# A second norm's end shared among three engines, a later last maximum, and a re-ordered first stage in an attention and mixture-of-experts kernel

## The chip, the cores and the metric

One core of a Trainium2 chip. The metric is device time in microseconds (us) of one execution. The kernel before took 849.73 us, the median of 3 runs (847.44 to 850.27).

## The reference, cut to what matters

x is [32, 256, 128] in fp32: 32 batches of 256 rows. The kernel holds it as 64 tiles of 128 rows.

```python
xn = layernorm(x)                                     # the first norm
q, k, v = split(xn @ w_qkv)                           # 16 heads of 8
attn = softmax(causal(q k^T / sqrt(8)))
y = (attn v) @ w_proj + b_proj + xn
a = (y - mean(y)) * rsqrt(var(y) + 1e-5) * gamma + beta   # the second norm
probs = softmax(xn @ Wr)                              # 8 experts, the best 2
f = sum over the best 2 of prob * (gelu(xn @ W1 + b1) @ W2 + b2)
out = x + a + f
```

## The kernel before

There are three stages. **The first** normalises x. VectorE takes moments of each tile (`tiles_moments`, `moments`), GpSimd raises the variance to -1/2 (L555) in the five column ranges of `MOMENTS`, and VectorE makes offsets. ScalarE normalises groups 0 to 11 (four tiles each, L729), VectorE groups 12 to 15 (L755). TensorE transposes each group; ScalarE takes the fp16 high part (L640), VectorE the low part (`low_group`, L760); TensorE multiplies by the router's weights (L1089). `step(0, 0)`, the q and k of batch 0, lies between. GpSimd then adds beta into x_all in eight pieces of eight tiles (L567), each as soon as its groups are normalised. `picks` finds the best two experts of each row and `places` gives each row a slot; both are chains of small VectorE operations, `places` after step 1. SyncE, in program order: the rows of q and k of batch 0 to DRAM (L462) and back re-laid (`load_half`: q_diag L437, k_cat L438), then in step 1 `fill_slots` (16 transfers of 598.5 KB that clear the slots in DRAM), two biases and two pieces of the experts' weights, and only then the q and k rows of step 1 (L462) and their return.

**The second** is software-pipelined attention: steps 1 to 35, of which a step s projects batch s (PROJECT), takes row maxima of batch s-1 (MAXIMA), exponentials of batch s-2 (SOFT), sums and the second norm's measures of batch s-3 (FINISH), and the norm's end of batch s-4 (LAST). Steps 4 to 23 are a hardware loop of two; from 24 (`TAIL`) they are written out, since they also load and split pieces of the experts' weights. In a step every engine follows the order of `USES`. Its end, before:

```python
("head", "onT", FINISH), ("wide1", "s3", SOFT), ("maxA", "m10", MAXIMA),
("wide0", "s4", SOFT), ("maxB", "m11", MAXIMA), ("head", "o0", SOFT),
("misc", "shift", MAXIMA), ("wide1", "s5", SOFT), ("head", "proj", FINISH),
```

The first word is the PSUM buffer: a use must wait until the one before it in that buffer has been read out. m0 to m11 are scores for maxima (TensorE L1127, L1131; VectorE reduces them, L911), s0 to s5 scores for exponentials (TensorE L1113, L1117; ScalarE L653; GpSimd masks them, L581), o0 and o1 the value products (TensorE L1148; ScalarE reads them out, L671), shift the transposed maxima (ScalarE L649, then four SyncE transfers, L478), oT0, oT1 and onT transposes, proj the output product (L1196). o0 needs masks s0 to s2, o1 (in the next step) s3 to s5. After proj VectorE runs `add_and_measure` (L936 to L945), GpSimd the -1/2 power (L608). VectorE's `last`, placed after shift, ends the norm of the batch before: two L951, y2 = (x2 - mean) * gamma, and two L957, x_all += y2 * rstd. GpSimd also sends rows to their slots (`send_tile`, two L572 a tile): from step 2 on one tile at "m0" and one at "s2"; in the tail every even step three, at "m0", "s1", "s3". At the end of step 3 VectorE runs `pack_experts` (L884 to L898). In the tail ScalarE takes the high part of a piece (L681) at the end of a step and VectorE the low part (L982) before `add_and_measure`.

**The third** runs 72 tiles of 256 slots through the experts and adds the parts to x_all, which goes out.

## Time and profile before

| | |
|---|---|
| median of 3 runs | 849.73 us |
| the profiled execution | 851.77 us |
| its span | 850.0 us |
| busy: PE / VectorE / ScalarE / GpSimd | 699.9 / 692.9 / 525.4 / 536.0 us |
| first stage to the last router product | 0 to 63.9 us |
| attention steps | about 64 to 558 us |
| experts' tiles, then the last sum | to 811 us, to 850 us |

Durations are of the one profiled execution; 1.77 us of its time lie outside its span. A row gives the start, the duration of the whole group (with xN for N instructions), the engine, the line, and in brackets the idle time before it and what ended that. A row's duration is longer than the spacing of neighbours where operations overlap at their ends. PE is TensorE, PEld its weight load, DVE VectorE, ACT ScalarE, POOL GpSimd, SPq the SyncE queue.

### The profile page before, as it was taken

How to read it: one execution, taken by the hardware profiler on the slowest of the kernel's cores; microseconds unless marked ns; L12 is line 12 of the kernel's file. 1: busy time of each engine (PE TensorE's matmuls, PEld its weight loads, DVE VectorE, ACT ScalarE, POOL GpSimd, SP SyncE). 2: the span in 40 equal slices, each digit the busy share in tenths (PEclk: the TensorE clock that was granted, in tenths of full speed). 3: DMA queues.
4: the chain of work that ended last, by engine and by line, in shares of the span. 5: the costliest groups of instructions: out<-in, count | busy, mean ns of one | idle time of the engine just before them, and what ended most of it. 6: DMA issues, size and time to landing. Idle time of an engine off the chain costs nothing.

```text
span 850.0 us, 24989 instructions
## 1 busy us (share of the span) xinstructions
PE 699.9 (82%) x7877; PEld 518.1 (61%) x7878; DVE 692.9 (82%) x1617; ACT 525.4 (62%) x1039; POOL 536.0 (63%) x575
## 2 busy tenths in 40 slices
PE   1366579999999999999888888868999999999800
PEld 1243346666666666666655555537888889888800
DVE  5778878898999998989889999557788888888744
ACT  4541346565656565656556565537989999999800
POOL 8750456767676776767777777334767676667710
PEclk9999899999999999999999999978999999999955
DMA  8294122232323232232233432202222222222189
GB/s 220 80 400 122 64 84 94 81 111 79 114 77 111 80 111 94 94 98 90 84 127 107 139 125 78 64 7 62 84 85 80 85 88 84 82 82 82 56 266 335
DMA packets 113313, 93.66 MB, mean 110 GB/s; under 512 B 16618, under 2 KB 97650, under 8 KB 113268
## 3 DMA queue, kind: packets, MB, share of 16 engines
q1 hardware_dynamic: 95508, 70.26, 27.0%
q0 software_dynamic: 8704, 18.17, 5.9%
q10 hardware_dynamic: 9056, 4.66, 1.9%
q8 instruction: 25, 0.41, 0.2%
q14 instruction: 20, 0.16, 0.1%
HBM read 43.85 MB, written 48.93 MB: 109 GB/s over the span
## 4 chain that ended last, share of the span: by engine, by line
PE 56%; DVE 13%; issue 7%; POOL 7%; DMA 6%; ACT 5%; SPq 5%; DVEq 0%; ACTq 0%; POOLq 0%
PE wide L1259 10%; PE bank_head L1148 7%; PE wide L1113 5%; PE bank_head L1250 5%; PE bank_maxB L1250 5%; PE bank_maxA L1127 4%; PE bank_maxB L1127 3%; DMA xn_rows<-parts_dram 3%; DMA k_cat<-qk_rows 3%; DVE shift L911 3%; POOL probs L581 3%; PE bank_misc L1173 3%; SPq L478 2%; PE bank_maxB L1131 2%; PE bank_maxA L1131 2%
## 5 line engine op out<-in xcount | busy, mean ns | idle before, releaser
L581 POOL TENSOR_SCALAR_AFFINE_SELECT probs<-probs 128x512 f32<-128x512 f32 (+1 forms) x192 | 158.3, 833 | 103.6 <-ACT probs L653 102.8
L653 ACT ACTIVATE probs<-wide 128x1024 f32<-128x1024 f32 x192 | 188.8, 1018 | 47.3 <-PE wide L1117 24.5
L619 POOL DMA_INDIRECT parts_dram<-o_T,dest x144 | 161.0, 1118 | 74.7 <-issue 48.6
L572 POOL DMA_INDIRECT x_slots<-xn_rows,slot_i x128 | 127.3, 995 | 62.8 <-DVE slot_i L868 31.4
L911 DVE TENSOR_REDUCE shift<-bank_maxA 128x2 f32<-128x512 f32 (+1 forms) x192 | 132.1, 688 | 20.1 <-PE bank_maxA L1131 12.9
L911 DVE TENSOR_REDUCE shift<-bank_maxB 128x2 f32<-128x512 f32 (+1 forms) x192 | 131.5, 685 | 4.9 <-PE bank_maxB L1131 0.8
L687 ACT ACTIVATE probs<-wide,b_all 128x256 f32<-128x256 f32 x288 | 121.4, 478 | 16.8 <-PE wide L1259 10.0
L1148 PE MATMUL bank_head<-probs,v_aug 128*32 128x256 f32 (+1 forms) x2048 | 98.9, 334 | 19.1 <-POOL probs L581 18.9
L1259 PE MATMUL wide<-xgT_raw,xnT 128*128 128x256 f16 x864 | 109.2, 277 | 3.7 <-DVE xgT_raw L1020 3.6
L1003 DVE TENSOR_TENSOR probs<-probs 128x512 f16<-128x512 f32 x144 | 99.7, 692 | 5.5 <-ACT probs L693 1.1
L1127 PE MATMUL bank_maxA<-k_cat,q_diag 128*128 128x128 f16 (+1 forms) x512 | 76.2, 252 | 28.5 <-DVE shift L911 19.5
L1148 PEld LDWEIGHTS bank_head<-probs,v_aug 128*32 128x32 f32 x2048 | 60.5, 111 | 56.2 <-issue 21.4
L1259 PEld LDWEIGHTS wide<-xgT_raw,xnT 128*128 x864 | 78.8, 99 | 16.4 <-issue 4.9
L671 ACT ACTIVATE o_T<-bank_head 128x512 f32<-128x512 f32 x64 | 38.2, 597 | 73.8 <-PE bank_head L1148 73.8
L1113 PE MATMUL wide<-q_diag,k_cat 128*128 128x512 f16 x256 | 76.9, 384 | 0.0
L1127 PE MATMUL bank_maxB<-k_cat,q_diag 128*128 128x256 f16 (+1 forms) x512 | 75.5, 250 | 0.3
L1127 PEld LDWEIGHTS bank_maxA<-k_cat,q_diag 128*128 128x128 f16 x512 | 36.7, 98 | 56.2 <-DVE shift L911 34.4
L1127 PEld LDWEIGHTS bank_maxB<-k_cat,q_diag 128*128 128x128 f16 x512 | 42.2, 99 | 30.3 <-DVE shift L911 8.0
L1131 PE MATMUL bank_maxB<-mask,ident 128*128 128x256 f16 (+1 forms) x192 | 60.5, 315 | 0.0
L1131 PE MATMUL bank_maxA<-mask,ident 128*128 128x256 f16 (+1 forms) x192 | 60.4, 314 | 0.0
L1250 PE MATMUL bank_head<-xnT,probs 128*128 x864 | 55.3, 220 | 0.0
L1250 PE MATMUL bank_maxB<-xnT,probs 128*128 x864 | 55.0, 219 | 0.2 <-DVE probs L1003 0.2
(174 smaller groups left out, 1252.4 us busy)
## 6 DMA issues: line engine op xcount, KB each, us to landing
qk_rows<-split SPq DMA_DIRECT2D x32, 512.0 KB, 3.2
x_slots<-fill SPq DMA_DIRECT2D x16, 598.5 KB, 7.6
fill<-x_slots SPq DMA_DIRECT2D x72, 133.0 KB
q_diag<-qk_rows SPq DMA_DIRECT2D x256, 32.0 KB
k_cat<-qk_rows SPq DMA_DIRECT2D x64, 128.0 KB
xn_rows<-parts_dram SPq DMA_DIRECT2D x8, 1024.0 KB, 11.8
x_all<-in_x SPq DMA_DIRECT2D x8, 512.0 KB, 7.6
pieces_f<-in_w SPq DMA_DIRECT2D x8, 512.0 KB, 4.8
```

The source lines that it names most:

```text
L572: pool.indirect_dma_start(out=x_slots, out_offset=bass.IndirectOffsetOnAxis(ap=slot_i[:, t, c:c + 1], axis=0), in_=xn_rows[:, t, :], in_of ...
L581: pool.affine_select(out=part, in_=part, compare_op=ALU.is_ge, fill=0.0, base=0, pattern=[[0, n], [1, P]], channel_multiplier=-1).then_inc ...
L619: pool.indirect_dma_start(out=parts_dram, out_offset=bass.IndirectOffsetOnAxis(ap=dest[:, of, t:t + 1].bitcast(U32), axis=0), in_=y[:, of ...
L653: act.activation(probs[:, u, :], ps[:, :], ACT.Exp, scale=SCALE).then_inc(empty, 1)
L687: act.activation(hT[:, par, c, :], wide[par][:, S * c:S * (c + 1)], ACT.Gelu, bias=b1_all[:, bass.ds(e, 1), c:c + 1].rearrange("p a b -> p ...
L911: V.tensor_reduce(dst, ps[:, :].rearrange("p (j k) -> p j k", j=nh), axis=AX.X, op=ALU.max, negate=True).then_inc(empty, 1)
L1113: last = M(ps[:, 512 * h2:512 * (h2 + 1)], keys[:, gs[0], :], q_diag[:, par, gs[0], 2 * h2:2 * h2 + 2, :], start=True, stop=True)
L1127: M(ps[:, keys * n_:keys * (n_ + 1)], q_diag[:, 1 - par, g, j, P * qt:P * (qt + 1)], k_cat[:, 1 - par, g, 0:keys], start=(n_ == 0), stop=F ...
L1131: M(dst, ident16[:, :], mask16[:, :].rearrange("p (o k) -> p o k", o=1).to_broadcast([P, nh, P]), start=False, stop=True, skip_group_check ...
L1148: last = M(dst, v_aug[:, of, kt, J * g + j, :], p_, start=(kt == 0), stop=(kt == 1), skip_group_check=True)
L1250: last = M(results[:, D * t:D * (t + 1)], hT_parts[:, par, hp, c, P * t:P * (t + 1)], w2_parts[:, wp_, bass.ds(e_2, 1), c, :].rearrange("p ...
L1259: last = M(wide[par][:, S * c:S * (c + 1)], w1_parts[:, wp_, bass.ds(e_1, 1), P * c:P * (c + 1)].rearrange("p a d -> p (a d)"), xgT[:, par ...
```

## The change

GpSimd's first memset of q_diag is split in two, the ranges of the moments become six (the third is eight tiles), ScalarE normalises 13 groups, VectorE three. `low_router` and `step(0, 0)` come later on VectorE. The router's and wqkv's weights have semaphores of their own, the router's are loaded first. The beta adds move: four pieces after `picks`, two at the end of step 2, two at the end of step 3. In `places` eight scans over 64 elements become one over 512, and four operations go into `weights`, at the end of step 2. Sends begin in step 3 and go on to step 32; an even tail step has two tiles at "m0", one at "s2". s5 comes before o0. At the end of a step ScalarE multiplies y2 by rstd (two operations) and GpSimd adds y2 into x_all (one of 128x256), in place of the two L957. High parts of pieces are taken right after v.

```diff
+        goes_on = probs[:, 5, 512:1024].rearrange("p (e t) -> p e t", e=E)
         is_top16, key16 = (probs[:, 4, NT * E // 2 * u:NT * E // 2 * (u + 1)].bitcast(BF16).rearrange("p (t e) -> p t e", e=E) for u in range(2))
         pick16 = probs[:, 5, 0:NT * E].bitcast(BF16).rearrange("p (c t e) -> p c t e", c=2, e=E)
         top = sb("top", [P, 2, NT])
@@ -169,6 +172,8 @@
...
@@ -240,7 +246,7 @@
 
...
-            ("wide0", "s4", SOFT), ("maxB", "m11", MAXIMA), ("head", "o0", SOFT),
-            ("misc", "shift", MAXIMA), ("wide1", "s5", SOFT), ("head", "proj", FINISH),
+            ("wide0", "s4", SOFT), ("maxB", "m11", MAXIMA), ("wide1", "s5", SOFT),
+            ("head", "o0", SOFT), ("misc", "shift", MAXIMA), ("head", "proj", FINISH),
...
-                places = ("m0", "s1", "s3") if (s - TAIL) % 2 == 0 else SEND_AFTER
+                places = ("m0", "m0", "s2") if (s - TAIL) % 2 == 0 else SEND_AFTER
...
-        ACT_GROUPS = 12
+        ACT_GROUPS = 13
...
-        MOMENTS = [(0, 8), (8, 16), (16, 32), (32, 48), (48, 64)]
-        assert NT == 64 and 4 * ACT_GROUPS == MOMENTS[-1][0]
...
+        MOMENTS = [(0, 8), (8, 16), (16, 24), (24, 40), (40, 56), (56, 64)]
...
-            pool.memset(q_diag[:, 0, :, :, :], 0.0).then_inc(consts, 1)
             for c, (begin, end) in enumerate(MOMENTS):
+                if c < 2:
+                    pool.memset(q_diag[:, 0, 2 * c:2 * c + 2, :, :], 0.0).then_inc(consts, 1)
...
+                elif c == 2:
                     pool.memset(q_diag[:, 1, :, :, :], 0.0).then_inc(consts, 1)
-                elif c == 2:
+                elif c == 3:
...
-            for c in range(BETA_PARTS):
+            pool.memset(goes_on[:, :, :], 1.0).then_inc(consts, 1)
...
+            pool.memset(goes_on[:, :, 0], 0.0).then_inc(consts, 1)
+
+            def add_beta(c):
                 tiles_ = slice(NT // BETA_PARTS * c, NT // BETA_PARTS * (c + 1))
-                wait_normed(pool, 2 * c + 1)
                 pool.tensor_tensor(x_all[:, tiles_, :], x_all[:, tiles_, :],
-                                   beta_bc[:, :].rearrange("p (o d) -> p o d", o=1).to_broadcast([P, NT // BETA_PARTS, D]), ALU.add).then_inc(offset_ready, 1)
+                                   beta_bc[:, :].rearrange("p (o d) -> p o d", o=1).to_broadcast([P, NT // BETA_PARTS, D]),
+                                   ALU.add).then_inc(offset_ready if c < BETA_PARTS - 1 else res_ready, 1)
+
+            wait_normed(pool, ACT_GROUPS - 1)
+            wait_normed(pool, GROUPS - 1)
+            pool.wait_ge(weights_loaded, 64)
+            pool.wait_ge(route, ROUTE_PICKED + 1)
+            for c in range(BETA_PARTS // 2):
+                add_beta(c)
...
-                    pool.wait_ge(route, ROUTE_DONE)
+                    pool.wait_ge(route, ROUTE_WEIGHTS)
...
+                if s in (2, 3):
+                    for c in range(2 * s, 2 * s + 2):
+                        add_beta(c)
+                if has(s, LAST):
+
+                    b = s - LAST
+                    pool.wait_ge(y2_scaled, b * QT + QT)
+                    mine = x_all[:, b * QT:(b + 1) * QT, :]
+                    pool.tensor_tensor(mine, mine, y2[:, :, :], ALU.add).then_inc(res_ready, 1)
...
-            act.dma_start(wqkv[:, :], w_qkv).then_inc(weights_loaded, 16)
+            act.dma_start(wr[:, :], w_router).then_inc(router_loaded, 16)
+            act.dma_start(wqkv[:, :], w_qkv).then_inc(qkv_loaded, 16)
             act.dma_start(wp[:, :], w_proj).then_inc(weights_loaded, 16)
-            act.dma_start(wr[:, :], w_router).then_inc(weights_loaded, 16)
...
-            act.wait_ge(weights_loaded, 96)
+            act.wait_ge(qkv_loaded, 16)
...
                         act.activation(v_aug[:, 1 - par, :, :, 0:HD],
                                        ps[:, 0:QT * D].rearrange("p (t h d) -> p t h d", t=QT, h=H), ACT.Copy).then_inc(empty, 1)
+                        for i in pieces(s):
+                            high_piece(i)
...
                         exp(s, int(what[1:]))
-                for i in pieces(s):
-                    act.wait_ge(piece_loaded[i % 2], 16 * (i // 2 + 1))
-                    act.activation(part_of(i, 0), piece[i % 2], ACT.Copy).then_inc(piece_high, 1)
+                if has(s, LAST):
+
+                    b = s - LAST
+                    act.wait_ge(rstd2_ready, b * 1 + 1)
+                    act.wait_ge(y2_ready, b * QT + QT)
+                    for t in range(QT):
+                        act.activation(y2[:, t, :], y2[:, t, :], ACT.Copy, scale=rstd2[:, t:t + 1]).then_inc(y2_scaled, 1)
...
-                then(V.tensor_scalar(xn_rows[:, :, D + 4], best[:, 0, :], -1.0, float(E), ALU.mult, ALU.add))
...
-                for e in range(E):
-                    V.tensor_tensor_scan(place[:, :, e], ones[:, :], total.rearrange("p (t e) -> p t e", e=E)[:, :, e],
-                                         padded[:, e:e + 1], ALU.mult, ALU.add).then_inc(route, 1)
-                    route_count += 1
-                dve.wait_ge(exp_router, 2)
-                then(V.tensor_reduce(red[:, :], prob[:, :, :], axis=AX.X, op=ALU.add))
...
+                then(V.tensor_tensor(first_tile_total, first_tile_total, padded[:, :], ALU.add))
+                dve.wait_ge(consts, 31)
+                then(V.tensor_tensor_scan(place_by_expert[:, :, :].rearrange("p e t -> p (e t)"), goes_on[:, :, :].rearrange("p e t -> p (e t)"), total, 0.0,
+                                          ALU.mult, ALU.add))
...
-                then(V.reciprocal(xn_rows[:, :, D], red[:, :]))
-                then(V.tensor_tensor(red[:, :], top[:, 1, :], xn_rows[:, :, D], ALU.mult))
-                then(V.tensor_tensor(xn_rows[:, :, D + 2], red[:, :], xn_rows[:, :, D], ALU.subtract))
...
+            def weights():
+
+                nonlocal route_count
+                dve.wait_ge(exp_router, 2)
+                then(V.tensor_reduce(red[:, :], prob[:, :, :], axis=AX.X, op=ALU.add))
+                V.tensor_scalar(xn_rows[:, :, D + 4], best[:, 0, :], -1.0, float(E), ALU.mult, ALU.add).then_inc(route, 1)
+                route_count += 1
+                then(V.reciprocal(xn_rows[:, :, D], red[:, :]))
+                then(V.scalar_tensor_tensor(out=xn_rows[:, :, D + 2], in0=top[:, 1, :], scalar=-1.0, in1=xn_rows[:, :, D],
+                                            op0=ALU.add, op1=ALU.mult))
...
+                if has(s, LAST):
+                    dve.wait_ge(y2_ready, (s - LAST) * QT + QT)
                 V.tensor_tensor(x2[:, :, :], ps[:, 0:QT * D].rearrange("p (t d) -> p t d", t=QT), xpb[:, :, :], ALU.add).then_inc(empty, 1)
...
+                dve.wait_ge(res_ready, b * 1 + 1)
                 for t in range(QT):
                     V.scalar_tensor_tensor(out=y2[:, t, :], in0=x2[:, t, :], scalar=mv2[:, t, 0:1], in1=gamma_bc[:, :],
                                            op0=ALU.subtract, op1=ALU.mult).then_inc(y2_ready, 1)
-                dve.wait_ge(rstd2_ready, b * 1 + 1)
-                for t in range(QT):
-                    dve.wait_ge(y2_ready, b * 2 + (t + 1))
-                    mine = x_all[:, bass.ds(b * QT + t, 1), :].rearrange("p a d -> p (a d)")
-                    V.scalar_tensor_tensor(out=mine, in0=y2[:, t, :], scalar=rstd2[:, t:t + 1], in1=mine,
-                                           op0=ALU.mult, op1=ALU.add).then_inc(res_ready, 1)
...
+                if isinstance(s, int) and s == SOFT:
+                    weights()
...
-            step(0, 0)
-            tiles_moments(56, 64)
...
-            dve.wait_ge(rstd_ready, 5)
...
+            low_group(5)
+            tiles_moments(56, 64)
+            offsets(4)
+            moments(5)
+            low_group(6)
+            step(0, 0)
+            low_group(7)
+            dve.wait_ge(rstd_ready, 6)
+            half_of_mean(ACT_GROUPS)
...
-            dve.wait_ge(offset_ready, BETA_PARTS)
...
+                for n_, (counting, order_) in enumerate(((after16, "p t e -> p (t e)"), (ones16, "p t e -> p e t"))):
...
+                        last = M(wide[1][:, 512 * n_:512 * (n_ + 1)], counting[:, :], pick16[:, c, :, :].rearrange(order_),
...
+            pe.wait_ge(weights_loaded, 64)
...
```

## Rows read from the trace of the kernel before

**Rows 1.** Windows, loop: PE, PEld, DVE, ACT, POOL busy us, clock, DMA share, GB/s.
```profile
190.00:414.00 224.00, 218.72 (x2372) 144.50 (x2370) 204.13 (x449) 138.31 (x193) 162.03 (x193) 1.00 0.30 96
```

**Rows 2.** Timeline, first stage, where the beta adds run.
```profile
36.30 9.24 POOL L567 TENSOR_TENSOR x_all<-x_all,beta_bc 128x1024 f32<-128x1024 f32 x4
38.71 7.16 DVE L755 TENSOR_SCALAR xn_rows<-x_all,mean,rstd 128x128 f32<-128x128 f32 x4
46.40 1.10 DVE L755 TENSOR_SCALAR xn_rows<-x_all,mean,rstd 128x128 f32<-128x128 f32 x4
```

**Rows 3.** Timeline, VectorE from picks to the first maxima of steps 1 and 2.
```profile
63.98 0.69 DVE L825 TENSOR_REDUCE top<-wide 128x64 f32<-128x512 f32 x1 [0.58 <-PE wide L1089]
71.41 0.69 DVE L911 TENSOR_REDUCE shift<-bank_maxA 128x4 f32<-128x512 f32 x1
84.27 2.02 DVE L850 TENSOR_TENSOR_SCAN probs<-ones,padded,wide 128x64 f32<-128x64 f32 x8
91.67 0.69 DVE L911 TENSOR_REDUCE shift<-bank_maxA 128x4 f32<-128x512 f32 x1
```

**Rows 4.** Timeline, SyncE's queue over the same time.
```profile
39.89 18.64 SPq L423 DMA_DIRECT2D x_slots<-fill  x16
...
66.79 2.01 SPq L416 DMA_DIRECT2D pieces_f<-in_w  x2
73.57 0.37 SPq L462 DMA_DIRECT2D qk_rows<-split  x1
76.36 1.75 SPq L437 DMA_DIRECT2D q_diag<-qk_rows  x4
```

**Rows 5.** Timeline, step 4: TensorE's wait while VectorE runs `pack_experts`.
```profile
125.09 0.39 PE L1127 MATMUL bank_maxA<-k_cat,q_diag 128*128 128x256 f16 x2 [3.89 <-DVE shift L911]
```

**Rows 6.** The chain that ended last, one step of the loop: start, us, what.
```profile
316.43 1.44 PE bank_head L1148 x32
317.86 0.32 PE bank_misc L1181 x2
318.18 0.43 PE wide L1117 x2
318.61 0.69 PE bank_head L1196 x4
...
324.03 0.39 PE bank_maxA L1127 x2
```

**Rows 7.** Timeline, ScalarE, GpSimd and VectorE in the same step.
```profile
315.38 1.94 ACT L653 ACTIVATE probs<-wide 128x1024 f32<-128x1024 f32 x2
317.93 0.60 ACT L671 ACTIVATE o_T<-bank_head 128x512 f32<-128x512 f32 x1 [0.61 <-PE bank_head L1148]
319.42 0.42 DVE L936 TENSOR_TENSOR x<-bank_head,xpb 128x256 f32<-128x256 f32 x1 [0.46 <-PE bank_head L1196]
319.81 1.09 POOL L581 TENSOR_SCALAR_AFFINE_SELECT probs<-probs 128x1024 f32<-128x1024 f32 x1 [0.37 <-ACT probs L653]
```

**Rows 8.** Waits from 95 to 420 us: total us, times, longest.
```profile
PEld bank_head L1196 <- ACT o_T L671: 10.3, 22, 0.5
PE bank_head L1148 <- POOL probs L581: 6.8, 21, 1.2
```

**Rows 9.** Groups: the first two from 190 to 414 us, the third over the span.
```profile
L957 DVE SCALAR_TENSOR_TENSOR x_all<-y,rstd,x_all 128x128 f32 x32 | 21.5, 710 | 0.0
L590 POOL TENSOR_TENSOR xpb<-xn_rows,bproj_bc 128x256 f32<-128x256 f32 x16 | 10.8, 678 | 0.0
L729 ACT ACTIVATE xn_rows<-x_all,offset,rstd 128x128 f32<-128x128 f32 x48 | 19.6, 483 | 2.5 <-DVE offset L800 2.5
```

**Rows 10.** Tail steps: the chain, then TensorE's timeline.
```profile
454.88 3.99 DMA k_cat<-qk_rows
...
479.28 1.51 PE L1148 MATMUL bank_head<-probs,v_aug 128*32 128x256 f32 x32 [1.07 <-POOL probs L581]
485.01 1.29 PE L1148 MATMUL bank_head<-probs,v_aug 128*32 128x256 f32 x24 [1.32 <-POOL probs L581]
```

More of the change, by code:

```diff
@@ L109, in attention_and_moe @@
         piece = (pieces_f32[:, 0, :], pieces_f32[:, 1, :])
-        others, place, rank, prob = (probs[:, u, 0:NT * E].rearrange("p (t e) -> p t e", e=E) for u in range(4))
+        others, place, rank = (probs[:, u, 0:NT * E].rearrange("p (t e) -> p t e", e=E) for u in range(3))
+        place_by_expert = probs[:, 3, 0:NT * E].rearrange("p (e t) -> p e t", e=E)
+        prob = sb("prob", [P, NT, E])
+        goes_on = probs[:, 5, 512:1024].rearrange("p (e t) -> p e t", e=E)
         is_top16, key16 = (probs[:, 4, NT * E // 2 * u:NT * E // 2 * (u + 1)].bitcast(BF16).rearrange("p (t e) -> p t e", e=E) for u in range(2))
@@ L171, in attention_and_moe @@
         x_loaded = [sem(f"x_loaded{c}") for c in range(2 * CHUNKS)]
+        router_loaded = sem("router_loaded")
+        qkv_loaded = sem("qkv_loaded")
         weights_loaded = sem("weights_loaded")
@@ L382, in attention_and_moe @@
         EXPERTS_PACKED = 16
[L383 to L385 removed]
+        ROUTE_DONE = 27
+        ROUTE_WEIGHTS = 31
+        MOMENTS = [(0, 8), (8, 16), (16, 24), (24, 40), (40, 56), (56, 64)]
+        assert NT == 64
         EARLY_AFTER = 4
@@ L653, in exp, with high_piece @@
                 act.activation(probs[:, u, :], ps[:, :], ACT.Exp, scale=SCALE).then_inc(empty, 1)
+            def high_piece(i):
+                act.wait_ge(piece_loaded[i % 2], 16 * (i // 2 + 1))
+                act.activation(part_of(i, 0), piece[i % 2], ACT.Copy).then_inc(piece_high, 1)
             def step(s, par):
@@ L839, in places @@
                 V.tensor_tensor(top[:, 1, :], top[:, 1, :], top[:, 0, :], ALU.subtract).then_inc(less_top, 1)
-                then(V.tensor_scalar(xn_rows[:, :, D + 4], best[:, 0, :], -1.0, float(E), ALU.mult, ALU.add))
                 dve.wait_ge(route_counts, 1)
                 total = wide[1][:, 512:1024]
-                then(V.tensor_reduce(padded[:, :], total.rearrange("p (t e) -> p e t", e=E), axis=AX.X, op=ALU.add))
+                then(V.tensor_reduce(padded[:, :], total.rearrange("p (e t) -> p e t", e=E), axis=AX.X, op=ALU.add))
                 then(V.tensor_scalar(padded_i[:, :], padded[:, :], float(S - 1), None, ALU.add))
@@ L1026, in tile, with half_of_mean @@
                     low_hidden(s - 1, 1 - par, 1)
+            def half_of_mean(c):
+                nonlocal prep_count
+                V.tensor_scalar(mean[:, 4 * c:], mean[:, 4 * c:], 0.5, None, ALU.mult).then_inc(prep, 1)
+                prep_count += 1
+                dve.wait_ge(prep, prep_count)
             tiles_moments(0, 8)
@@ L1034, in _ @@
             moments(1)
-            tiles_moments(16, 24)
+            tiles_moments(16, 20)
             offsets(1)
-            tiles_moments(24, 32)
+            low_router()
+            tiles_moments(20, 24)
             moments(2)
+            tiles_moments(24, 28)
             low_group(0)
+            offsets(2)
+            tiles_moments(28, 32)
+            low_group(1)
             tiles_moments(32, 40)
-            offsets(2)
-            low_group(1)
-            tiles_moments(40, 48)
             moments(3)
             low_group(2)
-            tiles_moments(48, 56)
+            tiles_moments(40, 48)
             offsets(3)
             low_group(3)
-            step(0, 0)
-            tiles_moments(56, 64)
+            tiles_moments(48, 56)
             moments(4)
             low_group(4)
-            dve.wait_ge(rstd_ready, 5)
-            cols = slice(*MOMENTS[4])
-            V.tensor_scalar(mean[:, cols], mean[:, cols], 0.5, None, ALU.mult).then_inc(prep, 1)
-            prep_count += 1
-            dve.wait_ge(prep, prep_count)
+            low_group(5)
[7 more added lines that the diff above has]
+            half_of_mean(ACT_GROUPS)
             for g in range(ACT_GROUPS, GROUPS):
                 normalise_group(g)
-                low_group(g - ACT_GROUPS + 5)
-            for g in range(GROUPS - ACT_GROUPS + 5, GROUPS):
+                low_group(g - ACT_GROUPS + 8)
+            for g in range(GROUPS - ACT_GROUPS + 8, GROUPS):
                 low_group(g)
             picks()
-            dve.wait_ge(offset_ready, BETA_PARTS)
             steps(dve, step, after=((), (places,)), first_tile=lambda: tile(0, 0, None))
             tiles(dve, tile, load=False, begun=1)
+            dve.wait_ge(res_ready, B + 1)
             for c in range(LAST_CHUNKS):
@@ L1096, in count_picks @@
                 pe.wait_ge(route, ROUTE_PICKED + 1)
-                for n_, counting in enumerate((after16, ones16)):
+                for n_, (counting, order_) in enumerate(((after16, "p t e -> p (t e)"), (ones16, "p t e -> p e t"))):
                     for c in range(2):
-                        last = M(wide[1][:, 512 * n_:512 * (n_ + 1)], counting[:, :], pick16[:, c, :, :].rearrange("p t e -> p (t e)"),
+                        last = M(wide[1][:, 512 * n_:512 * (n_ + 1)], counting[:, :], pick16[:, c, :, :].rearrange(order_),
                                  start=(c == 0), stop=(c == 1))
```

20 lines of the change are left out of this document (12 added, 8 removed).

## The prediction

> **What bounds it now.** I read the stages by windows first. In the loop of the attention steps [rows 1] 224 us hold sixteen steps, since the one xpb add of a step stands there 16 times [rows 9]: 14.0 us a step. TensorE is busy 218.72 us and VectorE 204.13; the reader should see that neither is plainly the bound. So I read the chain of one step [rows 6]: o0 takes 1.44 us from 316.43, the transposed maxima 0.32, s5 0.43, and proj starts at 318.61 and ends at 319.30. VectorE's L936 follows at 319.42 [rows 7], then measures, the maxima m0 and m1, the low parts of q and k, and m2, whose reduction frees buffer A; m4 starts at 324.03 [rows 6]. From m4 to the next proj all is TensorE. So the ring is: proj, 4.7 us of VectorE, m4, some 9.3 us of TensorE, proj. A second ring is nearly as long: o0, ScalarE's read-out, shift and exponential of s5, mask, o1; it shows in o1's 21 waits for the mask, 6.8 us together, 0.3 each [rows 8].
>
> Two facts of these rows decide about the change. VectorE already sits idle 0.46 us before L936, waiting for proj [rows 7]: work taken away ahead of that point is not on the ring. And proj is written into the buffer that o0 used, so it waits for ScalarE's read-out of o0: that runs from 317.93 to 318.53 [rows 7], and the weight load of proj waits for it in 22 steps of 22, 0.5 us each [rows 8]. Today shift and s5 run on TensorE in that time and hide it (they end at 318.61).
>
> The first stage loses time to the beta adds. Four VectorE normalisations take 7.16 us while they run, 1.10 without them [rows 2]. Behind it SyncE's queue is full: clearing the slots 39.89 to 58.53, pieces of weights to 68.80, q and k rows of step 1 at 73.57, their return from 76.36 [rows 4]; VectorE reaches the first maxima of step 2 only at 91.67 [rows 3].
>
> **The change, part by part.** The sum is made against 851.77 us, the profiled execution, which is 2.04 above the median of 849.73.
>
> **First stage.** Without the beta adds VectorE gets back about 8 us before 63.98 (6.1 in the four named, the rest in the twelve others) [rows 2, 3]. A memset halved before the first power, earlier weights, an eight-tile range and one group fewer on VectorE give some more; I estimate the last router product 10 to 17 us earlier, at 47 to 54. From there to the maxima of step 2 VectorE takes 91.67 - 63.98 = 27.7 us [rows 3]: picks, the maxima of step 1, places. It loses some 2 us in places, as `weights` leaves it, and wins 2.3 back if its copy in step 1 meets one beta add. The single scan: eight of 64 take 2.02 us; one of 512 reads as many elements, so 0.7 (one pass at the rate of the 128x512 reductions in rows 3) to 2.0; I take 1.5 plus an addition of 0.2, no saving, and it will have slack. VectorE would be ready at 75 to 82.
>
> But SyncE is not ready. `step(0, 0)` comes some 2 us later on VectorE, so the clearing starts at about 41.9; it and the loads behind it took 68.80 - 39.89 = 28.9 us [rows 4], with the transfers as the limit, so the queue is free at 70.8, and the rows of step 1 stand behind 1 MB of pieces. Their return can start at about 76.4, as now. k_cat is issued 1.8 us later and takes about 3: the first maxima of step 2 at 81.5 instead of 91.67. **Term: -10.2** (bounds -5, if VectorE is late, and -16, if the queue is quicker).
>
> **Beta adds, moved.** Four lie in step 1, under that wait: nothing. Two at the end of step 2 (4.7 us of GpSimd) meet `weights` and the copy of step 3: one stall of up to 2.3 us, partly where o1 now waits for a mask that comes earlier: +0.7. Two at the end of step 3 meet the measures' scalar operation and `pack_experts`, on which TensorE waits 3.89 us already [rows 5]. In rows 2 each VectorE operation of that kind lets one whole add pass, so two adds cost up to 4.6: +4.3. **Term: +5** (0 to 8). The Trainium skill has the mechanism (SBUF — State Buffer, Who interferes with whom): a VectorE operation in a two-port mode or with two SBUF inputs, and a GpSimd one that reads SBUF, exclude each other for a whole instruction, and a reduction doesn't take part. Rows 2 agree for tensor_scalar; by it the price here would be 4.6 as well, and not more, since only two adds are left.
>
> **Norm's end.** VectorE loses the two L957, 0.71 us each, 1.3 a step [rows 9]. In the loop that only lengthens its idle time ahead of L936: 0. ScalarE gets two of 0.48 (as L729) after the shift copy, ending before q and k come: 0, bounded by 1.0 a step if they don't fit. GpSimd gets one add of about 0.68 (as L590) [rows 9] between the mask of s5 and the power: 0, bounded by 0.7 if VectorE's small measure waits for it. The new wait ahead of L936 is one more instruction on the ring: +0.07.
>
> **s5 ahead of o0.** s5 needs only ScalarE's exponential of s3, done at about 316.4 [rows 7], so it starts at 316.43 and o0 0.43 later. o0 ends at 318.29; ScalarE, which now does s5 first, is free at 315.38 + 1.94 + 1.0 = 318.32. Read-out to about 318.97, proj from 319.04 instead of 318.61: **+0.43 a step**. The cover that s5 gave is gone, only shift (0.32) is left. The mask of s5, now ending at 319.81 + 1.09 [rows 7], comes 0.4 earlier, and o1's wait goes; but the ring over VectorE is the longer one and keeps its 4.7 us. With the wait above +0.5 in each of the 20 steps 4 to 23 and +0.4 in step 3: **+10.4** (0 to +12).
>
> **Tail, ten steps.** In about five the chain runs from o0 over the shift rows and SyncE to k_cat (3.99 us in the row) [rows 10]: these pay 0.43 too, +2.2. In even steps the sends at s1 and s3 delay the masks; o0 waits 1.07 and o1 1.32 [rows 10]. With both early tiles at m0 some 4 us go in all. Taking a piece's high part before s0 makes ScalarE wait for the piece where k_cat isn't late anyway: +1. **Term: -1** (-8 to +4). The later end of the sends (step 32) is before the tiles. Tiles and last sum: 0.
>
> Sum: -10.2 + 5 + 10.4 - 1 = **+4.2**, 856.0 for such an execution and **854 us** as a median.
>
> **The rivals.** (1) The step doesn't grow, and the kernel is **faster**. Place: proj's start in the loop. For it: o1's waits in 21 steps, and a PE that is busy 218.72 of 224. Against: the weight load's wait in all 22 steps. Sum -10.2 + 5 + 0 - 1 = -6.2: 843.5. It decides if a step grows by less than 6.2 / 20 = 0.31 us. (2) VectorE is the bound and each step gives its 1.3 us back. The Trainium skill says so for a saturated VectorE (Perfetto Trace Analysis, Optimizing Scalar/DVE Operations): give work to ScalarE, though it doubts GpSimd. Rows: 204.13 of 224 busy speak for it, the idle 0.46 before L936 against. -10.2 + 5 - 26 - 1: 818. (3) The first stage's gain passes on in full, -16: 848, about no change. Against: the full queue. (4) GpSimd's add or ScalarE's scaling does hold the next step, 0.5 more in 30 steps: +15 on top, 869. For the change not doing what it says: the norm's end does leave VectorE, and what is freed is idle time; that is the forecast.
>
> **Chances.** Forecast 0.52, of which a tenth of all lies inside 0.3% (2.5 us, about what a measurement of this kernel can tell from no change); (1) 0.24; (2) 0.04; (3) 0.11; (4) 0.09. Faster: (1) nearly all, (2), and a third of (3): 0.3. Same: 0.16. Slower: 0.54. The forecast's own range is 849 to 861. The range that should hold 8 in 10 takes (1) and (3) in and leaves (2) and (4) out: 843 to 862.
>
> **What would show it.** Right: first maxima of step 2 near 81.5; the step 14.5 us; proj's weight load waiting 0.7 us or more for L671 with TensorE idle; VectorE idle near 2 us before L936; no waits of o1 for the mask. Wrong: a step of 14.0 or less, or the first maxima of step 2 near 76 or 86, or masks, ScalarE's scaling or the y2 add ahead of a TensorE wait.

## The result, and the profile after

The changed kernel takes **860.73 us** (median of 4 runs, 859.35 to 862.11), the kernel before 849.25 beside it: ratio 1.0145, 95% interval 1.0116 to 1.0174. It is slower, and by 11.5 us, not by the 4.3 forecast. The time lies inside the range (843 to 862), near its upper end. One execution of e3 and one of the kernel before beside it took over 1210 us at a granted clock of 0.58, where all others had about 0.95; they are left out of what follows.

The profiled execution took 859.35 us, the lowest of the four, while that of before lies 2.5 above its median. So of the 11.5 us the two traces show 7.6 (spans of 857.6 and 850.0). Where these lie can be read from VectorE's add of the projection (L936 before, L987 after), once a step. Timeline of VectorE after, the adds of steps 4, 23 and 33:

```profile
133.15 0.42 DVE L987 TENSOR_TENSOR x<-bank_head,xpb 128x256 f32<-128x256 f32 x1 [1.99 <-PE bank_head L1254]
411.08 0.42 DVE L987 TENSOR_TENSOR x<-bank_head,xpb 128x256 f32<-128x256 f32 x1 [2.44 <-PE bank_head L1254]
563.65 0.42 DVE L987 TENSOR_TENSOR x<-bank_head,xpb 128x256 f32<-128x256 f32 x1 [0.85 <-PE bank_head L1254]
```

Before they stood at 137.59, 403.31 and 557.99. So the start gained 4.4 us; 19 steps of the loop take 277.93 us instead of 265.72, **14.63 each instead of 13.99**, +12.2; the ten tail steps take 152.57 instead of 154.68, -2.1; the rest 293.9 instead of 292.0, +1.9.

**The start.** Timeline after: SyncE's queue, then VectorE's first maxima of step 2 (91.67 before [rows 3]).

```profile
41.83 19.19 SPq L430 DMA_DIRECT2D x_slots<-fill  x16
...
70.61 0.37 SPq L469 DMA_DIRECT2D qk_rows<-split  x1
76.51 1.75 SPq L444 DMA_DIRECT2D q_diag<-qk_rows  x4
82.02 0.69 DVE L960 TENSOR_REDUCE shift<-bank_maxA 128x4 f32<-128x512 f32 x1 [5.84 <-PE bank_maxA L1189]
```

81.5 was forecast, and the cause is the one forecast: VectorE waits 5.84 us, and what comes late is SyncE's: the rows that step 1 stored at 70.61 are back only from 76.51 on. The gain of 9.65 us there is partly given back: 8.38 are left at the add of step 3 (118.12 before, 109.74 after), 4.44 at that of step 4. Timeline after, GpSimd's beta adds beside VectorE's measures, and TensorE behind them (3.89 before [rows 5]):

```profile
110.00 4.66 POOL L579 TENSOR_TENSOR x_all<-x_all,beta_bc 128x1024 f32<-128x1024 f32 x2
111.07 3.63 DVE L996 TENSOR_SCALAR mv<-mv 128x2 f32<-128x2 f32 x1
120.13 0.61 PE L1185 MATMUL bank_maxA<-k_cat,q_diag 128*128 128x256 f16 x2 [7.57 <-DVE shift L960]
```

**The loop.** Windows after (columns as in [rows 1]), then waits from 190 to 414 us, then one step of the chain that ended last:

```profile
190.00:414.00 224.00, 213.37 (x2275) 136.64 (x2274) 176.74 (x399) 140.53 (x216) 162.45 (x201) 1.00 0.28 90
```

```profile
PE bank_head L1254 <- ACT o_T L706: 6.4, 16, 0.4
PEld bank_head L1254 <- ACT o_T L706: 11.0, 16, 0.7
PEld wide L1175 <- ACT probs L682: 4.6, 15, 0.3
```

```profile
305.02 0.60 PE wide L1175 x2
305.62 1.48 PE bank_head L1206 x32
307.13 0.61 ACT o_T L706
307.78 0.73 PE bank_head L1254 x4
...
308.71 0.44 DVE x L987
```

The projection (L1254) waits for the read-out of o0 with TensorE idle, 0.40 us a step, as forecast. VectorE fell from 204.13 to 176.74 us of 224, or from 12.8 to 11.5 us a step, since fewer steps fit into the window. Hardly any of it came out as time: VectorE now stands idle 2.2 us a step ahead of L987 (35.0 us in 16), and the value products' waits for masks, 3.9 us in this window before, are gone. Of the 0.64 us a step, 0.36 is TensorE idle ((224 - 213.37) / 15.3 steps against (224 - 218.72) / 16) and the rest is longer busy; s5 takes 0.60 us where it took 0.43 [rows 6], since its weights now wait for ScalarE's exponential (the third wait above) and load in the open.

**The tail.** Waits of TensorE from 420 to 560 us, after; in before, o0 waiting for GpSimd's masks led there with 12.1 us:

```profile
PE bank_maxA L1185 <- DMA k_cat<-qk_rows: 7.3, 8, 1.7
PE bank_head L1206 <- POOL probs L601: 1.4, 2, 0.8
```

### The profile page after: what moved, and what is told of

The parts are those of the page before. It is cut to its first block, busy times and chain, and to the rows that moved or that the text cites. A ratio compares the mean times of both kernels' runs of the same rounds, so it can differ in the third digit from the quotient of the medians.

```text
span 857.6 us, 25019 instructions
## 1 busy us (share of the span) xinstructions
PE 709.3 (83%) x7876; PEld 513.6 (60%) x7878; DVE 654.2 (76%) x1549; ACT 545.0 (64%) x1107; POOL 558.1 (65%) x611
## 3 DMA queue, kind: packets, MB, share of 16 engines
q10 hardware_dynamic: 9056, 4.66, 1.8%
## 4 chain that ended last, share of the span: by engine, by line
PE 56%; DVE 12%; SPq 10%; DMA 8%; issue 6%; ACT 5%; POOL 2%; DVEq 1%; ACTq 0%; POOLq 0%
PE wide L1317 10%; PE bank_head L1206 6%; PE wide L1171 5%; PE bank_head L1308 5%; PE bank_maxB L1308 5%; PE wide L1175 4%; PE bank_maxA L1185 4%; DVE shift L960 3%; SPq L444 3%; DMA k_cat<-qk_rows 3%; PE bank_maxB L1185 3%; DMA xn_rows<-parts_dram 3%; SPq L485 3%; PE bank_misc L1231 3%; SPq L430 2%
## 5 line engine op out<-in xcount | busy, mean ns | idle before, releaser
L682 ACT ACTIVATE probs<-wide 128x1024 f32<-128x1024 f32 x192 | 185.8, 1023 | 37.6 <-PE wide L1171 18.9
L726 ACT ACTIVATE probs<-wide,b_all 128x256 f32<-128x256 f32 x288 | 121.5, 478 | 16.4 <-PE wide L1317 9.8
L1171 PE MATMUL wide<-q_diag,k_cat 128*128 128x512 f16 x256 | 76.3, 381 | 1.0 <-DMA q_diag<-shift_T 1.0
L696 ACT ACTIVATE split<-bank_misc 128x512 f16<-128x512 f32 x32 | 19.1, 597 | 65.4 <-PE bank_misc L1214 65.4
L987 DVE TENSOR_TENSOR x<-bank_head,xpb 128x256 f32<-128x256 f32 x32 | 13.6, 425 | 59.3 <-PE bank_head L1254 59.3
## 6 DMA issues: line engine op xcount, KB each, us to landing
fill<-x_slots SPq DMA_DIRECT2D x72, 133.0 KB
```

The lines of the kernel that those rows point to most:

```text
L682: act.activation(probs[:, u, :], ps[:, :], ACT.Exp, scale=SCALE).then_inc(empty, 1)
L726: act.activation(hT[:, par, c, :], wide[par][:, S * c:S * (c + 1)], ACT.Gelu, bias=b1_all[:, bass.ds(e, 1), c:c + 1].rearrange("p a b -> p ...
L1171: last = M(ps[:, 512 * h2:512 * (h2 + 1)], keys[:, gs[0], :], q_diag[:, par, gs[0], 2 * h2:2 * h2 + 2, :], start=True, stop=True)
```

## The experiments

All times are medians. "Step" is (add of step 23 - add of step 4) / 19, "tail" the time from the add of step 23 to that of 33, "rest" from there to the end of the span, each from the one profiled execution. The kernel before stood at 848.9 to 851.1 us in these comparisons; the ratios carry the verdicts.

| kernel | us | ratio to before, 95% | add of step 4 | step | tail | rest |
|---|---|---|---|---|---|---|
| before | 848.9 to 851.1 | | 137.6 | 13.99 | 154.7 | 292.0 |
| changed | 860.7 | 1.0145 (1.0116 to 1.0174) | 133.2 | 14.63 | 152.6 | 293.9 |
| e1 changed, order back | 843.3 | 0.9931 (0.9911 to 0.9951) | 133.0 | 14.05 | 150.2 | 295.2 |
| e2 changed, norm's end back | 860.4 | 1.0139 (1.0117 to 1.0162) | 132.8 | 14.72 | 153.7 | 290.9 |
| e3 before, new order | 867.6 | 1.0231 (1.0204 to 1.0257) | 139.8 | 14.72 | 154.9 | 290.7 |
| e4 before, new norm's end | 853.1 | 1.0056 (1.0036 to 1.0076) | 138.8 | 14.01 | 152.7 | 293.1 |
| e5 both back | 840.0 | 0.9887 (0.9861 to 0.9914) | 131.8 | 13.98 | 148.2 | 290.9 |
| e6 changed, projection's bank | 862.5 | 1.0149 (1.0122 to 1.0177) | 132.9 | 14.79 | 151.9 | 295.8 |
| e7 e1, projection's bank | 844.4 | 0.9923 (0.9894 to 0.9952) | 131.4 | 14.00 | 151.5 | 293.8 |
| e8 e1, beta adds early | 840.7 | 0.9896 (0.9872 to 0.9920) | 128.9 | 14.05 | 146.1 | 295.3 |
| e9 e6, shift first | 846.4 | 0.9950 (0.9928 to 0.9972) | 133.7 | 14.36 | 143.8 | 294.3 |
| e10 e5, beta early, k_cat first | 835.2 | 0.9828 (0.9802 to 0.9854) | 127.8 | 13.92 | 149.6 | 291.0 |
| e11 e10, start re-ordered | 832.2 | 0.9785 (0.9755 to 0.9815) | 126.0 | 13.91 | 148.8 | 290.0 |
| e12 changed, shift first | 864.9 | 1.0155 (1.0133 to 1.0178) | 134.4 | 15.17 | 146.8 | 295.0 |

**e1 to e4: which part costs.** e1 is this in the changed kernel, e3 the reverse of it in the kernel before:

```diff
-("maxB", "m11", MAXIMA), ("wide1", "s5", SOFT),
-("head", "o0", SOFT), ("misc", "shift", MAXIMA), ("head", "proj", FINISH),
+("maxB", "m11", MAXIMA), ("head", "o0", SOFT),
+("misc", "shift", MAXIMA), ("wide1", "s5", SOFT), ("head", "proj", FINISH),
```

> The changed kernel with the order of the step put back (s5 after o0 and shift), all else as changed. Theory A (the new order alone makes the step longer: the projection waits for the read-out of o0, and s5's weight load lies open): steps 4 to 23 take 13.95 to 14.05 us each instead of 14.63, the 8 steps of gain ahead of them stay (step 4's add of the projection near 133), the tail hardly moves, so about 848 us (846 to 850), within 0.3% of the kernel before and 1.4% below the changed one. Rival B (the new end of the norm, with its wait ahead of VectorE's add, makes the step longer): steps stay at 14.5 or more and the time at 858 or more. Rival C (both share it): 852 to 856.

> The kernel before with s5 put ahead of o0 in the order of the step, and nothing else. Theory A: steps grow from 13.99 to 14.55 to 14.65 us, over 20 steps and the tail 12 to 14 us, so 861 to 863 us (ratio 1.014 to 1.017); in the trace the projection waits for ScalarE's read-out of o0. Rival B (the order costs nothing without the new end of the norm): 849 to 851.

The order alone: 17.4 us back in e1, about 19 us lost in e3, and the step follows it both times (14.63 to 14.05, 13.99 to 14.72). Rival B falls. Both sizes were under-estimated. In the profiled executions they are 12.3 and 15.1: e1's profiled run was the highest of its six, and that of the kernel before lies above its median. e3's step of 14.72 is also 0.07 above the range expected.

e2 is this in the changed kernel, with ScalarE's waits and VectorE's wait for the differences ahead of its add of the projection gone too; e4 is the reverse in the kernel before:

```diff
-act.activation(y2[:, t, :], y2[:, t, :], ACT.Copy, scale=rstd2[:, t:t + 1]).then_inc(y2_scaled, 1)
...
-pool.wait_ge(y2_scaled, b * QT + QT)
-pool.tensor_tensor(mine, mine, y2[:, :, :], ALU.add).then_inc(res_ready, 1)
...
+dve.wait_ge(rstd2_ready, b * 1 + 1)
+V.scalar_tensor_tensor(out=mine, in0=y2[:, t, :], scalar=rstd2[:, t:t + 1], in1=mine,
+                       op0=ALU.mult, op1=ALU.add).then_inc(y2_scaled, 1)
```

> The changed kernel with the end of the second norm put back on VectorE (two multiply-adds of 0.7 us that add into x), the new order kept. Theory A (the order makes the step longer, VectorE idles 2 us ahead of the add of the projection): the two multiply-adds fill 1.4 of the 2 idle microseconds, steps stay at 14.55 to 14.65 and the time at 859 to 861. Rival B (the new end of the norm holds the step): steps fall to 14.0 to 14.2 and the time to 848 to 852.

> The kernel before with the new end of the second norm alone (ScalarE scales, GpSimd adds into x, VectorE's two multiply-adds gone, its add of the projection waits for the two differences), old order. Theory A: the step stays within 0.05 us of 13.99, the time 848 to 851 (ratio 0.999 to 1.002); GpSimd's add and ScalarE's two scalings hide. Rival B: ScalarE's two scalings at the end of its step (0.68 us) delay the next step's copies, steps of 14.2 or more and 854 or more. A third outcome, that VectorE was holding something and the step shortens to 13.9 or less (847 or less), would mean that the new order spoils a gain.

Within the new order the end of the norm changes nothing in sum (860.4 against 860.7). In the old order it costs 4.2 us (e4), although the step stays at 14.01, so neither theory A's total nor rival B's place is right. The "rest" column tells one part: it is 293.1 to 295.8 in the eight kernels with the new end of the norm and 290.0 to 292.0 in the six with the old one. Read from the last add of the projection (step 34) to the end of the span it is clearer still: 280.3 to 280.8 us with the new end, 277.6 to 277.9 with the old one, so the new end costs 2.4 to 3.2 us there.

In the new order this price is met by a gain in the loop: steps of 14.72 in e2 and e3 and 14.63 in the changed kernel. The traces show where it comes from. Timeline of VectorE in e2:

```profile
308.17 2.42 DVE L993 SCALAR_TENSOR_TENSOR x_all<-y,rstd,x_all 128x128 f32 x2
310.51 0.41 DVE L972 TENSOR_TENSOR x<-bank_head,xpb 128x256 f32<-128x256 f32 x1
```

In 7 of the 16 steps from 190 to 414 us the two multiply-adds take 2.4 us in all (1.3 in the others), here with three masks of GpSimd beside them, and VectorE comes to its add 0.36 us late with no idle time left; in the other nine it waits 1.1 us for the projection. So theory A's two idle microseconds were not enough in every step, which it had not expected.

Timeline of the last steps of the changed kernel, where the first tiles have begun:

```profile
577.12 0.42 DVE L987 TENSOR_TENSOR x<-bank_head,xpb 128x256 f32<-128x256 f32 x1 [2.02 <-PE bank_head L1254]
578.70 0.74 POOL L637 TENSOR_TENSOR rstd<-mv,half 128x2 f32<-128x2 f32 x1 [1.58 <-DVE mv L996]
579.47 0.69 ACT L720 ACTIVATE y<-y,rstd 128x128 f32<-128x128 f32 x2 [3.15 <-POOL rstd L637]
580.18 1.28 ACT L726 ACT_TABLE_LOAD   x1
...
582.21 0.38 ACT L741 ACTIVATE xgT_raw<-bank_misc 128x256 f16<-128x256 f32 x1
...
583.38 2.74 PE L1317 MATMUL wide<-xgT_raw,xnT 128*128 128x256 f16 x12 [4.82 <-DVE xgT_raw L1068]
```

ScalarE stands 3.15 us at the last scaling, which needs GpSimd's power of a value that VectorE has just made. Behind it are queued the loading of a function table (1.28 us) for the gelu of the first tile, that gelu (L726) and the read-out of the second tile (L741). From the last add of the projection to that tile's matmuls are 6.26 us here. With both parts put back (e5), the same rows:

```profile
557.56 1.28 ACT L713 ACT_TABLE_LOAD   x1
...
558.92 0.42 DVE L972 TENSOR_TENSOR x<-bank_head,xpb 128x256 f32<-128x256 f32 x1 [1.49 <-PE bank_head L1245]
...
560.40 0.38 ACT L728 ACTIVATE xgT_raw<-bank_misc 128x256 f16<-128x256 f32 x1 [0.71 <-PE bank_misc L1285]
...
562.88 2.74 PE L1308 MATMUL wide<-xgT_raw,xnT 128*128 128x256 f16 x12 [2.51 <-DVE xgT_raw L1059]
```

3.96 us: 2.3 us of the norm's price, for here the table is loaded before the last add, and not 3.06 us behind it. Of the 4.2 us in e4 some 1.5 were not located.

**e5: both back.**

> The changed kernel with both the order of the step and the end of the second norm put back: what is left of the change is the first stage, the moved beta adds, the routing and the places of the sends. Theory A (the new end of the norm costs 0.02 to 0.06 us per step by its waits, the order the rest): steps of 14.00 us, 839 to 843 us; the kernel before with the new end of the norm ran 4.2 us above the kernel before, and the same 4 us should go here. Rival B (the end of the norm is free beside the new sends, as it was beside the new order): 843 to 845.

840.0, 9.0 below before, 3.3 below e1: theory A in the time and in the step (13.98). But most of what the end of the norm costs lies behind the last add, as above, and not in its waits step by step: e1's step is 0.06 longer, 1.2 us in 19. This is what the first stage, the routing and the tail's sends are worth alone.

**e6, e7: is it the shared bank?**

```diff
-("head", "proj", FINISH),
+("maxB", "proj", FINISH),
```

> The changed kernel with the projection put into the PSUM bank of the odd maxima (free since m11) instead of o0's. Theory A (the projection waits for ScalarE's read-out of o0 only because both use one bank): that wait of 0.4 us a step goes, steps of 14.2 to 14.35 us instead of 14.63 and 852 to 856 us. Rival B (the wait comes back as one of m1 on VectorE's add of the projection, or of onT on the normalised heads): steps stay at 14.6 and the time at 859 to 861.

> The changed kernel with the order of the step put back and the projection in the bank of the odd maxima. In the kernel with the order put back the projection's weight load still waits 0.46 us a step for the read-out of o0. Theory A (that wait is open there as well): steps of 13.65 to 13.85 instead of 14.05, 836 to 840 us against 843.3. Rival B (it lies beside the matmul of s5, and its end costs nothing): 843 to 844; or m1 waits for the add of the projection and it becomes 846 or more.

Theory A, my own, falls in both: e7 (844.4, step 14.00) is where e1 was. In e6 the wait for o0's read-out is gone and the step is no shorter. Waits of TensorE from 190 to 414 us in e6:

```profile
PE bank_maxA L1185 <- DMA k_cat<-qk_rows: 10.5, 15, 0.9
PE bank_maxB L1185 <- DVE x L987: 3.8, 15, 0.3
```

0.7 us a step at m6, for the second half of k_cat. The second row, 0.25 us a step, is rival B's wait, which is there as well; e6 missed rival B's range too (14.79 for 14.6). The chain of e6 over one step shows a ring of its own:

```profile
310.15 0.36 ACT shift_T L678
...
310.58 0.59 SPq L485
...
314.96 2.67 DMA k_cat<-qk_rows
...
317.75 0.40 PE bank_maxA L1185 x4
```

ScalarE reads shift out at 310.15, SyncE issues four shift rows (0.6 us each), then the four loads of q_diag and the one of k_cat, and m6 starts 7.6 us after the read-out. From m6 to the next read-out of shift (324.82) are 7.1 us, and s5 and o0 are both in it; in the old order s5 came behind shift. Sum 14.67, within 0.12 of e6's mean step. The changed kernel over the same stretch (timeline):

```profile
307.62 0.36 ACT L678 ACTIVATE shift_T<-bank_misc 16x256 f16<-16x256 f32 x1
308.05 2.44 SPq L485 DMA_DIRECT2D q_diag<-shift_T  x4
...
312.44 0.43 SPq L445 DMA_DIRECT2D k_cat<-qk_rows  x1
315.24 0.39 PE L1185 MATMUL bank_maxA<-k_cat,q_diag 128*128 128x128 f16 x4
```

m6 comes 2.80 us after k_cat's issue, and 2.79 in e6, where it waits for it. That alone proves little. From 190 to 414 us this distance is 2.40 to 2.82 us in the changed kernel (mean 2.53), 2.50 to 2.94 in e6 (2.72) and 2.41 to 2.96 in e1 (2.57), whose step is 14.05. So I took the changed kernel for one that two rings hold at about the same length, of which only one shows as a wait; how much slack the second had there was not measured. The next two runs test it.

**e9, e12: the two rings apart.** The same edit, in e9 with the projection in maxB as well, in e12 in the changed kernel:

```diff
 ("wide1", "s5", SOFT),
-("head", "o0", SOFT), ("misc", "shift", MAXIMA),
+("misc", "shift", MAXIMA), ("head", "o0", SOFT),
```

> The changed kernel with the projection in the bank of the odd maxima (as in the run before) and shift put ahead of o0: m11, s5, shift, o0, projection. That run fell at 862 us: the wait for o0's read-out was gone and TensorE waited for k_cat instead. Theory D (two loops held the changed step at 14.6 to 14.7 us at once: the projection behind o0's read-out, and SyncE's queue, where shift's read-out, four loads of 0.6 us, the five loads of the second half of q and k and their landing take 7.2 us up to m6, and m6 to shift, o0 now among it, takes the rest): with shift 1.5 us earlier the second loop falls to 13.2 us, steps of 13.9 to 14.2, the tail 4 us or more below 152, so 840 to 850 us. Rival E (TensorE's own work and its waits for ScalarE and VectorE hold the step, and the wait for k_cat only took the place of slack): steps of 14.5 or more and 856 or more.

> The changed kernel with shift put ahead of o0 alone (m11, s5, shift, o0, projection, all in the banks of the changed kernel). It completes four cases: steps of 14.63 us with neither edit, 14.79 with the projection in another bank, 14.36 with both. Theory D (two loops, each able to hold 14.6 us): SyncE's loop is relieved, the one behind o0's read-out is not and loses the cover of shift's 0.4 us, so steps of 14.6 to 14.95, no shorter than the changed kernel's; the tail, where SyncE's loop alone holds, falls from 152.6 to 144 to 148; 854 to 864 us. Rival H (SyncE's loop alone was the cost of the new order): steps of 14.2 to 14.4, 842 to 848 us.

Waits of TensorE from 190 to 414 us, in e12 and then in e9:

```profile
PE bank_head L1254 <- ACT o_T L706: 10.8, 15, 0.7
```

```profile
PE bank_maxB L1185 <- DVE x L987: 4.0, 16, 0.3
PE bank_misc L1239 <- DVE shift L960: 1.5, 10, 0.2
```

Relieving either ring alone shortens nothing (14.79, 15.17), both together do (14.36), and theory D stands. e9 has the same wait of m1 as e6 and is 0.43 us shorter, so that wait is not what held e6. Neither edit is a pure relief, though: e12 also makes the ring over o0's read-out longer. Three numbers missed: e12's step is 0.2 above my range, for without shift as cover the projection waits 0.7 us (0.4 in the changed kernel) and shift now stands 0.2 us behind s5, by its place for m11's reduction; e12's time (864.9) is 0.9 above its range; and e9's step is 0.15 above. e9's tail, 143.8, is the shortest of all, where SyncE's ring led. What keeps e9 0.3 us above the old order (m1 behind the add, shift's wait, s5's open weight load) was not taken apart.

**e8, e10, e11: the start and the tail.** e8 is e1 with all beta adds behind the picks:

```diff
-for c in range(BETA_PARTS // 2):
+for c in range(BETA_PARTS):
     add_beta(c)
...
-if s in (2, 3):
-    for c in range(2 * s, 2 * s + 2):
-        add_beta(c)
```

> The changed kernel with the order of the step put back and all eight beta adds right behind the picks, where GpSimd sits idle, instead of four of them in steps 2 and 3. Theory A (the adds cost 4 to 5 us where they stand: VectorE's scalar operation took 3.63 us beside one, and the routing behind it stretched the step to 23.4 us): step 4's add of the projection near 129 instead of 133, 838.5 to 839.5 us. Rival B (the packing of the experts holds that step on its own): 842 to 844.

Step 4's add came at 128.93, 4.1 us earlier, as theory A had it; of these the median shows 2.6 (840.7, for 838.5 to 839.5). The same two rows in e8:

```profile
110.52 0.21 DVE L993 TENSOR_SCALAR mv<-mv 128x2 f32<-128x2 f32 x1
116.15 0.39 PE L1182 MATMUL bank_maxA<-k_cat,q_diag 128*128 128x256 f16 x2 [3.89 <-DVE shift L957]
```

Against the changed kernel 3.63 us became 0.21 and TensorE's wait 7.57 became 3.89. In e1, from which e8 differs by this edit alone, the adds began 0.16 us after that operation (0.23 us) had begun and met two of `pack_experts` instead, 1.45 and 2.23 us where e8 has 0.20 and 0.17; TensorE's wait was 7.16.

e10 is e5 with this and, in each half of the loads of q and k, another order:

```diff
+sp.dma_start(k_cat[:, par, gs, :], kr[:, gs, :]).then_inc(half_loaded[h], 16)
 for j in range(J):
     rows = slice(ROWS * j, ROWS * (j + 1))
     sp.dma_start(q_diag[rows, par, gs, j, :], qr[j, :, gs, :]).then_inc(half_loaded[h], 16)
-sp.dma_start(k_cat[:, par, gs, :], kr[:, gs, :]).then_inc(half_loaded[h], 16)
```

> The changed kernel with the order and the end of the norm put back, the eight beta adds behind the picks, and in each half of the loads of q and k the large k_cat ahead of the four small ones of q_diag. Without the last edit, by the runs so far (840.0, less 2.6 to 4.1 for the beta adds) 836 to 837.5 us. Theory D (in the tail the second half's loads end the wait ahead of m6, their last 2.5 to 3 us being k_cat's landing): k_cat lands some 1.7 us earlier and the small ones behind it decide, 0.4 to 1 us a step in the ten tail steps, so 829 to 834 us; steps 4 to 23 stay at 13.98. Rival E (the landing is bound by the bytes of the whole half, or GpSimd's masks hold the tail): 836 to 838.

835.2 lies between the two ranges, 0.8 below what the beta adds were to give and no more than the interval leaves open (0.9802 to 0.9854); the tail is not shorter (149.6, 148.2 in e5). Waits of TensorE from 420 to 560 us in e10:

```profile
PE bank_head L1194 <- POOL probs L601: 10.7, 9, 1.8
PE bank_maxA L1173 <- DMA q_diag<-qk_rows: 3.9, 4, 1.5
```

With the order and the norm's end put back the masks lead the tail (10.6 us in e5 as well, k_cat 2.6), and where the loads hold it, it is now q_diag that ends last, for 3.9 us. Of theory D the place holds and the gain doesn't come; of rival E the part on the masks holds. The chance in e10 was elsewhere: the early adds now run beside the routing. Timelines of VectorE in e10 and in e11:

```profile
70.48 2.26 DVE L867 TENSOR_SCALAR padded_i<-padded_i 128x8 int32<-128x8 int32 x1
72.77 2.26 DVE L868 TENSOR_SCALAR padded<-padded_i 128x8 f32<-128x8 int32 x1
81.96 0.69 DVE L944 TENSOR_REDUCE shift<-bank_maxA 128x4 f32<-128x512 f32 x1 [1.15 <-PE bank_maxA L1177]
```

e11 is e10 with the experts' loads (b1, b2_twice, two pieces) moved from behind the clearing of the slots to ahead of step 0, and

```diff
-for c in range(BETA_PARTS):
+for c in range(5):
+    add_beta(c)
+pool.wait_ge(route, ROUTE_DONE)
+for c in range(5, BETA_PARTS):
     add_beta(c)
```

> The kernel of 835.2 us with two edits in the first stage: the experts' biases and the first two weight pieces (9.4 us of SyncE's issuing, between the clearing of the slots and step 1's store of q and k) go ahead of step 0, and of the eight beta adds five stand behind the picks and three behind the routing's last casts, so that none runs beside VectorE's small scalar operations (1.05, 2.26 and 2.26 us there, 0.17 us each without an add). Theory F (step 2 starts when both SyncE's queue and VectorE are free): the store goes out at 61 instead of 70.6 and VectorE is ready at 76 instead of 81, so the first maxima of step 2 are read near 76.3 instead of 81.96 and the time is 829 to 831 us. Rival G (the clearing's own transfers or something else hold the store, or the loads ahead of step 0 delay the start): 834 to 838.

```profile
69.59 0.17 DVE L870 TENSOR_SCALAR padded_i<-padded_i 128x8 int32<-128x8 int32 x1
76.03 0.69 DVE L947 TENSOR_REDUCE shift<-bank_maxA 128x4 f32<-128x512 f32 x1 [0.29 <-DVE slot_i L892]
78.83 1.79 DVE L965 COPY split<-split 128x512 f16<-128x512 f16 x1
```

76.03 against the 76.3 expected, so theory F's mechanism holds; 832.2 against 829 to 831. Of the 5.9 us gained there step 4 keeps 1.8. 1.5 go where the late adds meet VectorE's copy (1.79 us where 0.28 is usual), 1.3 in the next store, whose loads come 4.98 us behind it (3.64 in e10); the rest was not located. SyncE's row in e11 holds a surprise:

```profile
60.87 1.13 SPq L464 DMA_DIRECT2D qk_rows<-split  x1
70.80 0.38 SPq L437 DMA_DIRECT2D k_cat<-qk_rows  x1
```

The store went out 9.7 us earlier, but the loads that wait for it came only 9.9 us behind it (5.9 in the changed kernel: 70.61 to 76.51). Rival G had this part: the store shares its queue with sixteen clearing transfers of 600 KB. The Trainium skill says that each DMA engine takes a ring's descriptors in order (DMA: Bandwidth & Descriptors, Queues, rings and completion order), and these rows agree; no run separates the order of the queue from the traffic of the clearing itself. e11 is the fastest version found, 2.15% below before and, by the two ratios, 3.5% below the changed kernel.

## Why the prediction was right, and where it was not

- **First stage, -10.2.** Right in place, cause and nearly in size: first maxima at 82.02 for 81.5, a gain of 9.65. Rival (3), the gain passing on in full, had them near 76.
- **Beta adds, +5.** Right. The stretch from step 3's add (118.12 before, 109.74 after) to step 4's grew from 19.47 to 23.41 us, +3.9, for the +4.3 forecast, and 1.27 us went before it for the +0.7 at the first two adds; e8 confirms the +3.9 by taking it away. The rule behind it, that each operation lets one whole add pass, is too simple: one operation stood 3.63 us over two adds here, and 4.34 in e6.
- **s5 ahead of o0, +10.4.** Right in sign and place, too small, and only half the mechanism. The wait of 0.40 is there, but the step grew by 0.64, not 0.5: 12.2 us in 19 steps. The step of the prediction that failed is "it starts at 316.43 and o0 0.43 later": s5 with its weights in the open takes 0.60. The order by itself costs 0.58 a step (e1) to 0.74 (e3), where 0.43 was forecast. What it did not see at all is the ring over SyncE and k_cat, into which s5 was moved as well; e6 and e12 show that either ring alone holds 14.6 us or more, so that curing the wait that the profile names brought nothing. The prediction priced that ring in the tail only ("these pay 0.43 too").
- **Norm's end, 0 and +0.07 a step.** Right for the loop in the old order (+0.03 in e4, +0.06 from e5 to e1), and rival (4), 0.5 a step, is out. In the new order it is -0.09, since there VectorE's multiply-adds are at times on the ring. Wrong behind the loop: the last scaling, with the table load behind it, costs 2.4 to 3.2 us there. "Tiles and last sum: 0" is the line that failed.
- **Tail, -1.** -2.1 measured. Masks shrank and k_cat took their place.
- **The sum.** Against one profiled execution +4.2 was forecast and +7.6 came: up to step 4 -4.4 (forecast -4.3, with what the order adds in step 3 and 4), 19 steps +12.2 (+9.5), tail -2.1 (-1), rest +1.9 (0). The two terms that were too small, the order and what lies behind the loop, make up the miss, and the range held it only because it was wide. The other 3.9 us up to the 11.5 of the medians are the two profiled runs' distances from their medians. Rival (1), in which the step doesn't grow, was priced at 843.5, and e1 measures 843.3. That close a hit is luck: in e1's trace the tail is 4.5 us shorter (forecast 1) and the rest 3.2 longer (0). Rival (2) is answered by e4: VectorE works 188.06 us of 224 instead of 204.13 at the same step, and nothing got faster.
- **The Trainium skill's rule on the shared port** (SBUF — State Buffer, Who interferes with whom) priced the beta adds here as rows 2 did, and the runs agree with it on what is held and what isn't: scalar operations 3.63 against 0.21 and 2.26 against 0.17 us, a copy 1.79 against 0.28, and reductions from PSUM unchanged at 0.69.

## What to carry to other kernels

When a step is moved in a software pipeline, list every ring that it enters or leaves, the queue of the DMA issuer among them, and not only the one whose wait the profile names: two rings of about equal length show as one, and curing it shows the other. Work taken from an engine that is idle ahead of its critical operation buys little, here 0.09 us a step at best, and the wait put in its place is paid where the pipeline drains and something new, here a table load, is queued behind it. Place long GpSimd adds where the other engine runs reductions from PSUM, not where it runs small scalar operations or copies.

## What the runs showed of the hardware that was not expected

- One GpSimd add of 2.3 us held a VectorE scalar operation on 8 elements a partition for 2.26 us instead of 0.17, and the next one again (e10). Beside two adds in a row (4.66 us) one operation on 2 elements stood through both: 3.63 us in the changed kernel, 4.34 in e6, 0.21 without them.
- Moving ScalarE's last scaling behind the last add put its table load of 1.28 us there too: it starts 3.06 us behind that add in the changed kernel, in e5 1.36 us ahead of it.
- A 512 KB store issued right behind sixteen transfers of 600 KB on one queue had its loads start 9.9 us later (e11), against 5.9 where 9.6 us of other issuing lay between (changed kernel).
- The profiled execution lay up to 3.8 us (0.45%) from its kernel's median (e1), as much as the effect of a whole part of this change; sums made between two traces need that said.
